# The order of SyncE's transfers in the first heads, and the tick tables of all background work, changed in an attention kernel with quantised feed-forward layers

## The chip, the core and the metric

The kernel runs on one core of a Trainium2 chip. Its time is the device time of one execution in microseconds, and the number given is the median of several runs. A core has five engines that run their own instruction streams and wait for one another by semaphores: TensorE (PE: matrix products and transposes, in the page also PEld, its weight loads), VectorE (DVE), ScalarE (ACT), GpSimd (POOL) and SyncE (SP), which here issues nearly all transfers between HBM and the on-chip memory.

## What is computed

Sixteen sequences of 512 rows by 128 columns go through three steps, each added to its input: half a feed-forward layer, attention with 16 heads of width 8, and half a feed-forward layer again. The feed-forward layer quantises its normed input and its weight in blocks of 32 to a grid of few values:

```
x = x + 0.5 * ffn(layernorm(x))
x = x + attn(layernorm(x))
x = x + 0.5 * ffn(layernorm(x))

# attn, for every head
scores = einsum('bhqd,bhkd->bhqk', Q, K) / sqrt(8)
mask   = sigmoid(tpms(position_q, position_k, phase[h]))
scores = scores + 0.3 * log(mask + 1e-06)
out    = einsum('bhqk,bhkd->bhqd', softmax(scores), V)

# ffn
scales = max(abs(block)) / 7.5
out    = (nearest_on_grid(block / scales) * scales) @ wd.T + bias
```

The mask depends on the head and the two positions alone, and so is the same for all sequences: 16 masks of 512 by 512, 1 MB each.

## The kernel before

**Batches, periods, heads, ticks.** The 16 sequences are four batches of four (NQ = QB = 4). A period is the attention of one batch: 16 heads, taken in the order of HEAD_ORDER (0, 8, 1, 2, 3, ...). Heads are counted through, m = 0 to 63, so head 16 opens period 1. A head has eight ticks, k = 0 to 7: for each of the four sequences j = k // 2 a half (pair = k % 2) of the keys. A period has 128 ticks, numbered through.

**A tick.** TensorE adds K times Q to the mask that already stands in a half of S_PS (`scores`, L1687), ScalarE takes the exponential of 1024 columns from it into E (`exp_step`, L803). In the odd ticks TensorE also multiplies a block of the head before with the values (`weighted`, L1705). In ticks 6 and 7 VectorE copies the next head's mask into the two halves of S_PS (`seed`, L1254), each after the exponential that frees the half. The passage from tick 7 to tick 0, with these copies, is called the seam here.

**Transfers of a head.** SyncE runs `head(m)` for each head: it loads the mask of head m + 1 (`load_mask`, L473, 1 MB, into one of two buffers LNM), its stack, six transfers of parts of K and Q (`load_stack`, L413 and L416, 672 KB together), and the two shift rows of the softmax (`load_shift`, L426). The stack of head m + 1 may be loaded when the scores of head m - 1 are done, its mask when head m is seeded. The last piece of a stack to be issued is the shift rows.

**The masks.** They are computed once, in the opening, in the order of MASK_ORDER, and are put where there is room: STAGE gives each a place in BIG, in memory that later belongs to something else. `store_mask(h)` (L458) brings mask h to HBM. What reuses the place waits for it: the exponentials of head 1 for masks 9 to 12, `load_mask(3)` for mask 8 (it stands in the buffer of the odd heads), the first `o_norm` for 13 and 14, the load of batch 2's rows for 15. Masks 0 and 8 are used in place by heads 0 and 1.

**Background work.** While a batch is in its period, the next two are prepared and the one before is finished, and each step of this is placed by a table: the step is issued in the tick that the table names, on its engine (the ending `_pe`, `_act`, `_ve`). FIRST prepares batch 1 in period 0, LATE the batches after it (in two halves), CHAINS gives the tick at which the chain of each sequence j starts and SECOND (CLOSE in period 0, APART in 1 and 2) the steps of a chain as distances from it, LAST the work after the attention. In a chain the normed rows are turned (`turn_pe`, TensorE), copied (`xnt_act`, ScalarE), multiplied to Q and K (`q_pe`, `k_pe`), copied again with their bias (`q_act`, `k_act`), split into three parts by VectorE and GpSimd (`hi_q_ve`, `mid_q_ve`, ...) and bounded (`norms_k_pe` to `bound_act`). LAST and LATE hold the layer norms and quantisation: statistics, `lnexp_act` and `rstd_ve` (three small instructions of VectorE, L1054 to L1056), `centre_ve` (subtract the mean, L1081), `reduce_ve`, `scales_ve`, `to_grid_ve`, `from_grid_ve`, then turn, copy, product and add. GpSimd has no table: it takes its steps in a fixed order, each as soon as what it waits for is there; its bias adds (L606) wait for the centring.

**What sets the order within a tick.** TensorE takes the background of ticks 0 and 1 ahead of the tick's scores, and that of ticks 2 to 7 behind the scores and values of the tick; so a step at tick 7 and one at tick 0 of the next head stand at the same place unless others are there. ScalarE takes it behind the exponential. VectorE has no tick of its own but the seeds: it works through what the tables name, in order, and only the seeds tie it to the other two.

## Time and profile before

| what | us |
|---|---|
| median of 3 runs | 866.96 |
| lowest and highest | 866.51, 867.02 |
| the profiled execution | 868.58 |
| its span | 866.7 |
| PE busy in the span | 730.6 (84%) |
| ACT busy | 645.3 (74%) |
| DVE busy | 560.7 (65%) |
| POOL busy | 190.4 (22%) |

The profiled execution has its own time, of which the span is the part between its first and last instruction. TensorE, busy for 84% of the span, reads as busy by modelled ends, so the share alone doesn't tell how near to its limit it is. The chain that ended last goes by PE for 48% of the span, by DVE for 23%, by ACT for 14%, by transfers for 2%.

### The profile page before, as it was taken

What the parts mean: (1) busy time and instruction counts of PE and PEld (TensorE: products, weight loads), DVE (VectorE), ACT (ScalarE), POOL (GpSimd) and SP (SyncE); (2) the same over time, 40 slices, a digit from 0 to 9 for tenths busy, and PEclk for the clock granted to TensorE, in tenths of its full rate; (3) what the DMA queues carried; (4) which work ended last, traced back from release to release, by engine and by line L of the source; (5) the groups of instructions that cost most, each with busy time, mean ns of one, the idle gap of its engine ahead of it and who ended that gap; (6) DMA issues with size and microseconds to landing.
All of it is one profiled execution on the core that took longest, in us unless ns stands there. A gap on an engine that the chain in (4) does not pass through costs nothing.

```text
span 866.7 us, 12515 instructions
## 1 busy us (share of the span) xinstructions
PE 730.6 (84%) x4195; PEld 247.8 (29%) x4195; DVE 560.7 (65%) x1385; ACT 645.3 (74%) x759; POOL 190.4 (22%) x163
## 2 busy tenths in 40 slices
PE   0575727899998999999999999999998998999935
PEld 0142311232232323332332233223311331331224
DVE  8968877466999646899774466886433457332274
ACT  1557596588887888878878888887888887888711
POOL 0405662003344203163140031441200002000011
PEclk9995956899999999999999999999999999999986
DMA  5527769874666674756867548668675556456101
GB/s 148 123 83 316 251 201 364 257 221 134 216 221 197 196 216 152 214 174 165 261 192 238 166 123 233 204 170 252 202 231 182 173 172 195 142 185 212 43 0 54
DMA packets 56075, 162.08 MB, mean 187 GB/s; under 512 B 14130, under 2 KB 24506, under 8 KB 45586
## 3 DMA queue, kind: packets, MB, share of 16 engines
q1 hardware_dynamic: 51780, 154.37, 58.0%
q0 software_dynamic: 1776, 5.93, 2.1%
q10 hardware_dynamic: 2446, 0.89, 0.5%
q8 instruction: 36, 0.59, 0.3%
q14 instruction: 37, 0.30, 0.1%
HBM read 117.86 MB, written 43.29 MB: 186 GB/s over the span
## 4 chain that ended last, share of the span: by engine, by line
PE 48%; DVE 23%; ACT 14%; issue 10%; DMA 2%; SPq 1%; POOL 1%; DVEq 0%; ACTq 0%; POOLq 0%
PE S_PS L1687 18%; PE O_PS L1705 17%; ACT BIG L803 10%; DVE S_PS L1254 7%; PE F_PS L1586 4%; PE F_PS L1581 2%; DMA BIG<-shift_rows 1%; ACT BIG L851 1%; PE R_PS L1715 1%; PE P_PS L1623 1%; DVE ST L981 1%; DVE SC L1091 1%; DVE BIG L1081 1%; PE P_PS L1581 1%; PE P_PS L1586 1%
## 5 line engine op out<-in xcount | busy, mean ns | idle before, releaser
L803 ACT ACTIVATE BIG<-S_PS 128x1024 f32<-128x1024 f32 x512 | 507.9, 1023 | 125.3 <-PE S_PS L1687 122.4
L1687 PE MATMUL S_PS<-BIG 98*128 98x512 bf16 x1024 | 313.0, 390 | 46.5 <-DVE S_PS L1254 19.7
L1254 DVE COPY S_PS<-BIG 128x512 f32<-128x512 f32 x256 | 159.6, 687 | 183.7 <-ACT BIG L803 181.5
L1705 PE MATMUL O_PS<-BIG,VXP 128*18 128x512 f32 (+2 forms) x2048 | 271.8, 604 | 0.0
L1687 PEld LDWEIGHTS S_PS<-BIG 98*128 98x128 bf16 x1024 | 79.2, 98 | 315.2 <-ACT BIG L803 138.6
L629 POOL TENSOR_TENSOR XDT<-PART 128x512 bf16<-128x512 f32 x24 | 28.8, 1200 | 296.2 <-ACT PART L766 296.2
L1705 PEld LDWEIGHTS O_PS<-BIG,VXP 128*18 128x18 f32 (+2 forms) x2048 | 34.3, 95 | 99.8 <-issue 96.0
L606 POOL TENSOR_TENSOR X<-X,BFH 128x512 f32<-128x512 f32 x16 | 24.0, 1527 | 146.6 <-DVE BIG L1081 117.2
L844 ACT ACTIVATE BIG<-S_PS,TEMP 128x1024 f32<-128x1024 f32 x32 | 34.2, 1111 | 20.2 <-PE S_PS L1880 19.6
L606 POOL TENSOR_TENSOR BIG<-BIG,BFH 128x512 f32<-128x512 f32 x16 | 19.9, 1274 | 122.9 <-DVE BIG L1081 110.9
L645 POOL TENSOR_TENSOR PART<-PART 128x512 bf16<-128x512 f32 x28 | 36.5, 1305 | 37.0 <-DVE PART L1162 37.0
L1880 PE MATMUL S_PS<-PART 36*128 36x512 bf16 (+1 forms) x32 | 14.7, 577 | 29.7 <-DMA PART<-trig_parts 27.6
L638 POOL TENSOR_TENSOR PART<-PART 128x512 f32<-128x512 f32 x28 | 35.1, 1252 | 13.2 <-DVE PART L1156 9.8
L735 ACT ACTIVATE XDT<-F_PS 128x512 f32<-128x512 f32 x38 | 22.5, 593 | 17.8 <-PE F_PS L1581 17.8
L1586 PE MATMUL F_PS<-WDT,XDT 128*128 128x128 f32 x208 | 32.2, 302 | 0.0
L1586 PEld LDWEIGHTS F_PS<-WDT,XDT 128*128 128x128 f32 x208 | 28.1, 207 | 12.6 <-ACT XDT L735 7.3
L851 ACT ACTIVATE BIG<-BIG,CON 128x2048 f32<-128x2048 f32 x16 | 30.7, 1988 | 0.0
L1581 PE MATMUL F_PS<-IDENT,BIG 128*128 128x128 f32 x112 | 17.9, 284 | 14.4 <-DVE BIG L1117 10.2
L1156 DVE CAST PART<-PART 128x512 bf16<-128x512 f32 x28 | 22.8, 813 | 5.1 <-ACT PART L766 4.4
L988 DVE TENSOR_SCALAR VE<-MV 128x4 f32<-128x4 f32 x48 | 22.7, 473 | 1.6
L729 ACT ACTIVATE RS<-VE 128x8 f32<-128x8 f32 (+1 forms) x19 | 4.0, 209 | 25.5 <-DVE VE L988 18.2
L981 DVE BATCH_NORM_STATS2 ST<-X 128x6 f32<-128x128 f32 x96 | 20.9, 280 | 0.6
(197 smaller groups left out, 745.2 us busy)
## 6 DMA issues: line engine op xcount, KB each, us to landing
BIG<-ln_masks SPq DMA_DIRECT2D x62, 1024.0 KB, 6.3
ln_masks<-BIG SPq DMA_DIRECT2D x16, 1024.0 KB, 6.2
BIG<-q_parts SPq DMA_DIRECT2D x63, 192.0 KB
BIG<-k_parts SPq DMA_DIRECT2D x63, 144.0 KB
BIG<-q_parts SPq DMA_DIRECT2D x63, 128.0 KB
q_parts<-PART SPq DMA_DIRECT2D x9, 768.0 KB, 3.8
k_parts<-PART SPq DMA_DIRECT2D x18, 384.0 KB, 4.4
BIG<-k_parts SPq DMA_DIRECT2D x63, 96.0 KB
```

The source lines that it names most:

```text
L606: pool.tensor_tensor(Y, Y, bias[:, None, :].to_broadcast((128, T, H)), ALU.add).then_inc(s[name], 1)
L638: pool.tensor_tensor(F_, F_, hi, ALU.subtract).then_inc(s[f"{q}_r1"], 1)
L645: pool.tensor_tensor(P_[2], F_, P_[1], ALU.subtract).then_inc(s[f"{q}_lo"], 1)
L803: act.activation(E[:, m % 2, j, 2 * pair:2 * pair + 2, :], S_PS[:, pair, :, :], ACT.Exp, scale=LOG_WEIGHT)\
L844: act.activation(stage(h)[:, 1024 * pair:1024 * pair + 1024].rearrange("p (k l) -> p k l", l=L), S_PS[:, t % 2, :, :], ACT.Sigmoid, scale= ...
L851: act.activation(a, a, ACT.Ln, bias=CON[:, 1:2]).then_inc(s["ln_mask"], 1)
L981: c(ve.bn_stats(ST[:, k, QB * j + t, :], xj[:, t, :]), wait=False)
L1254: ve.tensor_copy(S_PS[:, pair, i, :], LNM[:, slot, 2 * pair + i, :]).then_inc(s["seeded"], 1)
L1581: mm = pe.transpose(dst[:, 128 * t:128 * t + 128], src[:, t, :], IDENT[:, :])
L1586: mm = pe.matmul(dst[:, 128 * t:128 * t + 128], lhsT[:, 128 * t:128 * t + 128], rhs[:, :], start=True, stop=True)
L1687: mm = pe.matmul(S_PS[:, pair, i, :], KT[0:ALL_ROWS, slot, K_COL[j], 128 * kb:128 * kb + 128], QT[0:ALL_ROWS, slot, j, :], start=False, st ...
L1705: mm = pe.matmul(O_PS[32 * j:32 * j + ahead + HD + 1, :], VXP[:, slot_of(n), at - ahead:at + HD + 1], E[:, m % 2, j, kb, :], start=kb == 0 ...
```

## The change

It changes tables and the order of SyncE's calls; no instruction is added or removed, and what is computed is the same.

```diff
+AFTER = {1: (8,), 2: (13, 14), 3: (15,)}
...
-CHAINS = ((43, 59, 75, 91), (3, 27, 51, 75), (3, 27, 51, 75), ())
-APART = dict(norm_ve=-2, turn_pe=0, xnt_act=1, q_pe=5, q_act=5, ...
-CLOSE = APART | dict(k_pe=9, k_act=9, hi_k_ve=10, mid_k_ve=14, v_pe=13, v_ve=14)
+CHAINS = ((43, 59, 75, 91), (3, 27, 51, 83), (3, 27, 51, 91), ())
+CLOSE = dict(norm_ve=-2, turn_pe=3, xnt_act=3, q_pe=5, q_act=4, ...
+APART = dict(norm_ve=-2, turn_pe=0, xnt_act=0, q_pe=4, q_act=5, ...
...
                 if more and m >= 1:
                     load_mask(m + 1)
-                    if m == 1:
-                        for h in range(13, 15):
-                            store_mask(h)
                     load_stack(sp, m + 1)
                     if i < NH - 1:
                         load_shift(sp, m + 1)
-                if m == 2:
-                    store_mask(15)
-                    sp.wait_ge(s["val_ready"], 2 * HALF_TILES)
-                    load_x(3)
-                if m == 3:
+                for h in AFTER.get(m, ()):
+                    store_mask(h)
+                if m == 4:
                     lnm_stored(sp, 15)
                     load_x(2)
+                if m == 5:
+                    sp.wait_ge(s["val_ready"], 2 * HALF_TILES)
+                    load_x(3)
...
             store_mask(0)
 
-            store_mask(9)
-
             sp.wait_ge(s["bound_copied"], 1)
...
             load_stack(sp, 1)
-            store_mask(10)
+            store_mask(9)
             load_shift(sp, 1)
-            store_mask(11)
-            store_mask(12)
-            store_mask(8)
+            for h in range(10, 13):
+                store_mask(h)
```

On SyncE, from the store behind stack 1 to the load of mask 3 (`ln_masks<-BIG` is a store of a mask, `BIG<-ln_masks` a load, `k_parts`, `q_parts` and `shift_rows` are a stack). Before:

```order
L458 DMA ln_masks<-BIG 128x2048
L426 DMA BIG<-shift_rows 2x4x512
L458 DMA ln_masks<-BIG 128x2048 x3
L473 DMA BIG<-ln_masks 128x2048
L458 DMA ln_masks<-BIG 128x2048 x2
L413 DMA BIG<-k_parts 48x1536
L416 DMA BIG<-q_parts 48x2048
L413 DMA BIG<-k_parts 32x1x1536
L416 DMA BIG<-q_parts 32x1x2048
L413 DMA BIG<-k_parts 16x1x1536
L416 DMA BIG<-q_parts 16x1x2048
L426 DMA BIG<-shift_rows 2x4x512
```

After, with that file's line numbers (465 stores, 480 loads a mask, 420, 423 and 433 are the stack):

```order
L465 DMA ln_masks<-BIG 128x2048
L433 DMA BIG<-shift_rows 2x4x512
L465 DMA ln_masks<-BIG 128x2048 x3
L480 DMA BIG<-ln_masks 128x2048
L420 DMA BIG<-k_parts 48x1536
L423 DMA BIG<-q_parts 48x2048
L420 DMA BIG<-k_parts 32x1x1536
L423 DMA BIG<-q_parts 32x1x2048
L420 DMA BIG<-k_parts 16x1x1536
L423 DMA BIG<-q_parts 16x1x2048
L433 DMA BIG<-shift_rows 2x4x512
L465 DMA ln_masks<-BIG 128x2048
```

The two stores between the load of mask 2 and stack 2 (masks 13 and 14) are gone from there, and one store (mask 8) stands behind the stack. The first store is mask 10 before and 9 after, the three behind the shift rows are 11, 12 and 8 before and 10 to 12 after. The stores of 13 and 14 follow stack 3, that of 15 stack 4, the load of batch 2's rows stack 5 and of batch 3's rows stack 6; before, batch 3's followed stack 3 and batch 2's stack 4.

On ScalarE in head 16, the first of period 1, behind head 15: `PART<-P_PS` without BQK is the copy of the turned rows, `OTS<-O_PS` the copy of finished outputs that opens head 17. Before:

```order
L803 ACTIVATE BIG<-S_PS 128x1024 x8
L735 ACTIVATE PART<-P_PS 128x512
L803 ACTIVATE BIG<-S_PS 128x1024 x3
L812 ACTIVATE OTS<-O_PS,CON 128x512
L803 ACTIVATE BIG<-S_PS 128x1024
L766 ACTIVATE PART<-P_PS,BQK 128x512
```

After:

```order
L739 ACTIVATE PART<-P_PS 128x512
L807 ACTIVATE BIG<-S_PS 128x1024 x4
L816 ACTIVATE OTS<-O_PS,CON 128x512
L807 ACTIVATE BIG<-S_PS 128x1024
L770 ACTIVATE PART<-P_PS,BQK 128x512
```

The copy stands one exponential earlier, behind tick 3 and no more behind tick 4; TensorE's turn stays behind tick 3. Period 2 has the same at its opening.

On VectorE in period 3, from the statistics of head 53 to the seeds for head 55 (`COPY S_PS<-BIG`; L1081 is the centring, L1091 the reduction). Before:

```order
L988 TENSOR_SCALAR VE<-MV 128x4
L1254 COPY S_PS<-BIG 128x512 x4
L1081 TENSOR_TENSOR BIG<-BIG,MV 128x2048
L1054 TENSOR_TENSOR RS<-RS 128x16
L1055 SCALAR_TENSOR_TENSOR RS<-RS,VE 128x16
L1056 SCALAR_TENSOR_TENSOR RS<-RS 128x16
L1091 TENSOR_REDUCE SC<-BIG 128x64
```

After:

```order
L992 TENSOR_SCALAR VE<-MV 128x4
L1085 TENSOR_TENSOR BIG<-BIG,MV 128x2048
L1258 COPY S_PS<-BIG 128x512 x4
L1095 TENSOR_REDUCE SC<-BIG 128x64
L1058 TENSOR_TENSOR RS<-RS 128x16
L1059 SCALAR_TENSOR_TENSOR RS<-RS,VE 128x16
L1060 SCALAR_TENSOR_TENSOR RS<-RS 128x16
```

The centring stands ahead of the seeds for head 54, and the reduction ahead of the three rstd instructions.

Of the other moves, those of which more is said below, by period and tick (k is the tick in the head):

| step | engine | before | after |
|---|---|---|---|
| period 0, four chains: turn, copy | PE, ACT | k = 3, 4 | k = 6, 6 |
| period 0: copy of Q | ACT | k = 0 of the next head | k = 7 |
| period 1: turns of `turn_pe` 18 and `turn_xd_pe` 82, 98 | PE | k = 2 | 17, 81, 97, k = 1 |
| period 2: turns of 18, 82, 90 | PE | k = 2 | 15, 80, 87, k = 7, 0, 7 |
| periods 1, 2: last chain starts | all | 75 | 83, 91 |
| periods 1, 2: `norms_q_pe` | PE | k = 6 | k = 5 |
| period 2, head 38: centring, rstd | DVE | 49, 50 | 50, 49 |
| period 3: `add_ve` of the third sequence | DVE | 33, head 52 | 31, head 51 |

## Rows read from the trace of the kernel before

**Rows 1.** The page's part 5, the costliest group.
```profile
L803 ACT ACTIVATE BIG<-S_PS 128x1024 f32<-128x1024 f32 x512 | 507.9, 1023 | 125.3 <-PE S_PS L1687 122.4
```
**Rows 2.** Windows: length; busy us (instructions) of PE, PEld, DVE, ACT, POOL; clock, DMA, GB/s.
```profile
240.00:260.00 20.00, 19.29 (x115) 7.34 (x113) 18.05 (x56) 16.47 (x24) 8.48 (x8) 1.00 0.68 212
...
720.00:740.00 20.00, 16.97 (x96) 3.52 (x88) 18.39 (x24) 14.35 (x16) 4.98 (x4) 0.91 0.56 175
```
**Rows 3.** Timeline of SyncE's queue, 127 to 143: start, us, instruction, tiles, count.
```profile
127.23 0.44 SPq L458 DMA_DIRECT2D ln_masks<-BIG  x1
...
128.40 3.81 SPq L458 DMA_DIRECT2D ln_masks<-BIG  x3
132.74 0.75 SPq L473 DMA_DIRECT2D BIG<-ln_masks  x1
133.55 2.69 SPq L458 DMA_DIRECT2D ln_masks<-BIG  x2
136.29 1.41 SPq L413 DMA_DIRECT2D BIG<-k_parts  x1
...
142.37 0.64 SPq L426 DMA_DIRECT2D BIG<-shift_rows  x1
```
**Rows 4.** The chain of waits in order of time: start, us, what.
```profile
142.37 12.48 DMA BIG<-shift_rows
```
**Rows 5.** Transfers by line in 127:136, 132:152, 169:192.5; issue to landing.
```profile
L458 SPq DMA_DIRECT2D ln_masks<-BIG x6: 440/1250/1403, 127.2 to 134.8; - x6
DMA to landing us min/median/max: 5.9/9.0/15.0
...
L473 SPq DMA_DIRECT2D BIG<-ln_masks x3: 468/752/2656, 132.7 to 151.7; - x3
DMA to landing us min/median/max: 12.1/15.0/20.4
...
L473 SPq DMA_DIRECT2D BIG<-ln_masks x3: 338/338/877, 169.5 to 191.9; - x3
DMA to landing us min/median/max: 5.0/9.6/13.8
```
**Rows 6.** Timeline of TensorE where heads 2, 4 and 7 start; last: idle before, releaser.
```profile
154.90 1.89 PE L1687 MATMUL S_PS<-BIG 98*128 98x512 bf16 x4 [7.55 <-DMA BIG<-shift_rows]
...
178.61 0.60 PE L1687 MATMUL S_PS<-BIG 98*128 98x512 bf16 x2
...
210.30 0.60 PE L1687 MATMUL S_PS<-BIG 98*128 98x512 bf16 x2
```
**Rows 7.** Timelines of TensorE and ScalarE in head 16.
```profile
316.82 0.66 PE L1581 MATMUL P_PS<-IDENT,XC 128*128 128x128 f32 x4
...
320.43 0.60 PE L1687 MATMUL S_PS<-BIG 98*128 98x512 bf16 x2 [0.58 <-ACT BIG L803]
...
318.86 0.59 ACT L735 ACTIVATE PART<-P_PS 128x512 f32<-128x512 f32 x1
```
**Rows 8.** Timeline of TensorE, first score products of heads 46 and 47.
```profile
642.11 0.89 PE L1687 MATMUL S_PS<-BIG 98*128 98x512 bf16 x2 [0.52 <-DVE S_PS L1254]
...
651.79 0.89 PE L1687 MATMUL S_PS<-BIG 98*128 98x512 bf16 x2 [0.53 <-DVE S_PS L1254]
```
**Rows 9.** Timeline of VectorE in head 38.
```profile
557.77 2.29 DVE L1081 TENSOR_TENSOR BIG<-BIG,MV 128x2048 f32<-128x2048 f32 x1
...
561.46 1.21 DVE L1054 TENSOR_TENSOR RS<-RS 128x16 f32<-128x16 f32 x1
```
**Rows 10.** Timeline in period 3: product of head 51, rstd of 54, seam and values of 55.
```profile
700.53 1.16 PE L1586 MATMUL F_PS<-WO,XDT 128*128 128x128 f32 x8
...
724.56 0.17 DVE L1054 TENSOR_TENSOR RS<-RS 128x16 f32<-128x16 f32 x1
...
731.73 0.89 PE L1687 MATMUL S_PS<-BIG 98*128 98x512 bf16 x2 [1.87 <-DVE S_PS L1254]
...
733.96 1.93 PE L1705 MATMUL O_PS<-BIG,VXP 128*27 128x512 f32 x8
```

More of the change, by code:

```diff
@@ new lines @@
+LATE = ((dict(stats_ve=(49, 52), lnexp_act=59, rstd_ve=60, centre_ve=64, reduce_ve=67, scales_ve=68, to_grid_ve=73,
+              from_grid_ve=77, turn_pe=(81, 87), xd_copy_act=(83, 89), ffn_pe=(84, 93), add_ve=(85, 93), stats1_ve=(90, 96),
+              lnexp1_act=98, rstd1_ve=98),
+         dict(stats_ve=(82, 83), lnexp_act=87, rstd_ve=91, centre_ve=97, reduce_ve=99, scales_ve=100, to_grid_ve=106,
+              from_grid_ve=106, turn_pe=(109, 118), xd_copy_act=(109, 118), ffn_pe=(112, 120), add_ve=(113, 122),
+              stats1_ve=(113, 122), lnexp1_act=123, rstd1_ve=125)),
+        (dict(stats_ve=(26, 27), lnexp_act=31, rstd_ve=32, centre_ve=33, reduce_ve=35, scales_ve=36, to_grid_ve=42,
+              from_grid_ve=42, turn_pe=(47, 58), xd_copy_act=(47, 58), ffn_pe=(54, 60), add_ve=(53, 61), stats1_ve=(57, 66),
+              lnexp1_act=68, rstd1_ve=75),
+         dict(stats_ve=(76, 81), lnexp_act=83, rstd_ve=86, centre_ve=89, reduce_ve=91, scales_ve=91, to_grid_ve=96,
+              from_grid_ve=99, turn_pe=(110, 118), xd_copy_act=(110, 118), ffn_pe=(113, 120), add_ve=(113, 121),
+              stats1_ve=(114, 122), lnexp1_act=125, rstd1_ve=123)))
@@ L125 @@
-LAST = ({}, AMID, AMID, ALONE)
+LAST = ({},
+        dict(turn_pe=(10, 17, 25, 31), at_act=(10, 18, 26, 34), out_pe=(12, 20, 28, 36), add_ve=(13, 21, 29, 37),
+             stats_ve=(16, 24, 29, 43), lnexp_act=45, centre_ve=51, rstd_ve=51, reduce_ve=56, scales_ve=60, to_grid_ve=64,
+             from_grid_ve=72, turn_xd_pe=(75, 81, 86, 97), xd_copy_act=(75, 81, 87, 97), ffn_pe=(77, 83, 92, 100),
+             add_ffn_ve=(77, 85, 91, 101)),
+        dict(turn_pe=(10, 15, 26, 34), at_act=(10, 18, 26, 34), out_pe=(12, 20, 30, 36), add_ve=(13, 21, 27, 37),
+             stats_ve=(18, 24, 32, 40), lnexp_act=49, centre_ve=50, rstd_ve=49, reduce_ve=56, scales_ve=57, to_grid_ve=65,
+             from_grid_ve=72, turn_xd_pe=(75, 80, 87, 98), xd_copy_act=(75, 80, 87, 98), ffn_pe=(77, 84, 94, 100),
+             add_ffn_ve=(75, 85, 96, 97)),
+        dict(turn_pe=(14, 22, 30, 38), at_act=(14, 22, 30, 38), out_pe=(15, 24, 32, 39), add_ve=(18, 25, 31, 40),
+             stats_ve=(18, 26, 36, 42), lnexp_act=51, centre_ve=43, rstd_ve=51, reduce_ve=48, scales_ve=54, to_grid_ve=58,
+             from_grid_ve=62, turn_xd_pe=(62, 70, 78, 86), xd_copy_act=(62, 70, 78, 86), ffn_pe=(64, 72, 80, 88),
+             add_ffn_ve=(67, 75, 85, 92)))
```

39 lines of the change are left out of this document (11 added, 28 removed).

## Prediction

> **What bounds the kernel now.** I read the page's busiest groups first, then the windows, then the chain of waits, then the timelines of the places where the change moves something. The costliest group is the exponentials, 512 of 1.02 us, eight to a head (L803), whose idle time ends with TensorE's scores (L1687) [rows 1]. A head on which nothing else lies takes 9.68 us, from its first score product at 642.11 to the next one at 651.79 [rows 8]. 64 such heads are 620 us of the span of 866.7 us. The rest is the opening, the ending, the background work of the other batches, and one hole: at 154.90 TensorE takes up head 2 after 7.55 us without work [rows 6], and the chain of waits puts the 12.48 us before it on the load of the shift rows, which is the last piece of that head's stack [rows 4].
>
> Why was that load late? SyncE issued it at 142.37 [rows 3], behind a queue: stores of masks 10 (127.23), 11, 12 and 8 (three from 128.40), the load of mask 2 (132.74), stores of 13 and 14 (133.55), then the stack (136.29). The landings come in that order. The last of the six stores was issued at 134.8 and landed 15.0 us later, at 149.8; mask 2's load landed at 132.7 + 12.1 = 144.8 [rows 5]. So two stores took 5.0 us of queue, 2.5 each, and the stack another 5.1 (149.8 to 154.9).
>
> **The stall (term A).** The new order has no store of 13 and 14 ahead of stack 2, and mask 8's store goes behind it; mask 9's store comes in after stack 1 instead, so mask 2's load has the same number of stores ahead since 127 and should land at 144.8 as now. Stack 2 can be issued when head 0's scores are done, about 134.8, and lands at 144.8 + 5.1 = 149.9: 5.0 us earlier. But the stores are only moved, and the queue has to carry them later. From the mask loads: mask 3 landed at 143.1 + 15.0 = 158.1 and mask 4 at 151.7 + 20.4 = 172.1; mask 5 at 169.5 + 13.8 = 183.3 and mask 6 at 180.7 + 9.6 = 190.3 [rows 5]. Between the last two lie one stack and one load, 7.0 us. Between the first two lie a stack, a store and two loads, 14.0 us, which leaves about 8 for a stack and a load. I take 7.5 for a head (3.5 the load, 4.0 the stack) and 3.5 for a batch of x, which has a mask's size. The new queue after stack 2 at 149.9 is then: mask 8 stored, 152.4. SyncE stands in mask 3's load until that has landed, and behind it stand stack 3, the stores of 13 and 14, and all later loads. The fastest load of the rows takes 5.0 us, so mask 3 lands at 157.4 and stack 3 at 161.4. Masks 13 and 14 to 166.4, head 4's pair to 173.9; mask 15 and head 5's pair to 183.9; batch 2 of x and head 6's pair to 194.9; batch 3 of x and head 7's pair to 205.9. Heads 4 and 7 now start at 178.61 and 210.30 [rows 6]. So of the 5.0 us, 4.7 are left at head 4 and 4.4 at head 7. From head 8 on the queue has no extra transfers, and with heads of 10.6 us (178.61 to 210.30 is three) it regains 3 us in each. **A = 4.4 us**; from 2.8 (below) to 5.5, if the stack takes 4.6.
>
> The other waits on the moved transfers are covered: head 1's exponentials need stores 9 to 12, which land at the places where 10, 11, 12 and 8 land now (133.1 for the first, 127.2 + 5.9 [rows 5]), and one tick's pair of score products and exponentials later each; the first o_norm needs 13 and 14 in head 4, 10 us after they land.
>
> **The tick tables.** In a period TensorE and ScalarE alternate. A background step costs what it adds to the engine that is late. Three kinds of moves count.
>
> *Copy right behind its turn.* In head 16, TensorE turns the normed rows at 316.82 (0.49 us to the next start), but ScalarE copies them only after one more exponential, at 318.86, and TensorE then stands 0.58 us before the score product at 320.43 [rows 7]. With the copy one tick earlier it lies in the time in which ScalarE waits for the turn anyway. That gives 0.5 us for the first chain of batches 2 and 3 each; the other chains stand beside a product of 1 us that covers the copy, and I take nothing for them. In batch 1's four chains the turn goes to tick k = 6, the copy beside it, and the Q copy into the gap at the head's end.
>
> *Turns into the head's seam.* At the seam TensorE waits for VectorE's mask copies: 0.52 us before the first score product of head 46, and again between its products [rows 8]. A turn (about 0.45 us) set at k = 7, 0 or 1 fills that; at k = 2 it is paid. With the last chain moved away (75 to 83 and 91), period 1 has three such turns (of 17, 81, 97) and period 2 three (15, 80, 87): 1.3 us each.
>
> *VectorE's order.* Centring 2048 columns takes 2.29 us, and it sets off GpSimd's bias adds; the small rstd step behind it then takes 1.21 us [rows 9], where the same instruction takes 0.17 us alone [rows 10]. In head 38 the new order puts the three rstd steps ahead of the centring. In head 54, centring, rstd, reduction and scales all stand between two seeds, and the seeds for head 55 are late: TensorE waits 1.87 us instead of 0.53, and then a group of value products takes 1.93 us, the granted clock of the slice being 0.91 [rows 2, 10]. The new order centres in head 53, where VectorE has room.
>
> Sums. **B**, period 0 behind head 7: four chains at 0.6 us at most, 2.4. But the first is under the queue's limit above, and the others lie where VectorE is busy 18.05 of 20 us [rows 2] with the same work as now, so 1.0 (0 to 2.4). **C**, period 1: 0.5 + 1.3 + 0.6 for head 28's late seed, whose chain steps go to head 28 and 29: 2.4 (0 to 4). **D**, period 2: 0.5 + 1.3 + 0.9 (head 38's 3 us of VectorE bring about 0.4 at the seam, and norms_q one tick earlier 0.5): 2.7 (0 to 3.5). **E**, period 3: 1.3 + 0.9 for the slow clock, less 0.8 for a new wait: an add now stands between the two pairs of seeds for head 52 and waits for a product that TensorE runs after head 51's last scores and values. That product took 1.16 us at 700.53 [rows 10]; with the add behind it the second pair comes some 1.3 us later than now, and the seam's own wait of 0.5 covers a part. 1.4 (-0.8 to 2.2).
>
> 4.4 + 1.0 + 2.4 + 2.7 + 1.4 = 11.9 us. The profiled execution took 868.58 us, 1.9 more than its span, and the median of the runs is 866.96, 1.6 below it. 868.6 - 11.9 = 856.7 for a profiled run, so **855.1 us** in the median.
>
> **A rule on GpSimd.** The seeds and casts that the tables move meet GpSimd's work at other moments. The rstd instruction at 1.21 and 0.17 us [rows 9, 10] shows what one such meeting costs: 1 us. The Trainium skill (GPSIMD Engine Reference, section Specifications) says that GpSimd's interfaces to SBUF are shared with VectorE and contend with its instructions that have two SBUF inputs; by that rule, which these rows bear out, every reordering may lose as well as win. Ten more such meetings before seeds that are already late would cost 10 us and undo B to E; that is why their lower ends are at 0.
>
> **Rivals.** *Only the stall pays* (0.16): VectorE is the bound of periods 0 to 2 and what TensorE saves returns as waiting for seeds. For it: seeds that follow VectorE's work without a gap before heads 10, 12, 13, 22, 23. Against it: heads 16, 32 and 54, where VectorE or ScalarE is free. 866.96 - 4.4 = 862.6.
>
> *The stack passes the stores anyway* (0.12): if the stack's late landing is its own and not the queue's, only SyncE's earlier issue counts: the shift rows go out some 2.8 us before 142.37 (two stores of 1.3 us each, and less waiting). A = 2.8 or less, with B to E cut by a third: 859. The Trainium skill (DMA: Bandwidth & Descriptors, Queues, rings and completion order) says that completion is not first-in first-out for an issuing engine, since a transfer may use fewer rings than another. The nine landings above are all in the order of issue, which speaks against it here.
>
> *All of it pays* (0.17): the upper ends, and the clock does not fall at head 2: 5.5 + 2.0 + 3.5 + 3.3 + 2.2 = 16.5, 850.5.
>
> *The queue falls behind* (0.05, slower). Place: SyncE waiting in mask 3's load for mask 8's store, with everything for heads 3 to 7 behind it. Price: six stacks at 5.1 instead of 4.0 and seven loads at 4.3 instead of 3.5 add 12 us, and head 7 starts 7.6 us later than now; with B to E at nothing the time is 874. It decides from head 7's stack landing after 210.3 plus what B to E bring; at 7.5 of those it would only be 867.
>
> *Nothing measurable* (0.03): half of that, or A undone by B to E.
>
> **How the numbers follow.** The forecast has 0.47. A measurement of this kernel can tell about 0.2% (1.7 us) from no change. Faster: 0.47 + 0.16 + 0.12 + 0.17 = 0.92; same 0.03; slower 0.05. The range reaches from the full case to the one where only the stall pays: 849.5 to 863.5.
>
> **What would show it.** After: head 2's first score product near 149.9 with under 3 us of idle before it; mask 3's load issued near 152 and not at 143; heads 4 and 7 at 173.9 and 205.9. In head 16 no wait of 0.58 us at its end. Head 54 to 55 with 0.5 us of wait and full clock; a wait of VectorE between the seeds of head 52. I am wrong if head 2 still waits over 4 us, if heads 3 to 7 wait for shift rows beyond these times, or if the seeds of periods 1 and 2 come later than now.

## Result and the profile after

| | median, us | lowest and highest | profiled execution | its span |
|---|---|---|---|---|
| before, 5 runs | 867.02 | 866.51, 872.70 | 868.58 | 866.7 |
| after, 5 runs | 855.03 | 849.15, 856.45 | 849.15 | 846.9 |

The ratio is 0.9846, with a 95% interval of 0.9814 to 0.9879: faster by 1.5%. The changed kernel was measured twice more among the experiments, with ratios of 0.983 (0.9803 to 0.9858) and 0.9831 (0.9804 to 0.9858), so some 12 to 15 us. Its profiled execution is the shortest of its five, 5.9 us under their median, and is no measure of the whole; its parts are compared below with two further profiles.

From the page of the changed kernel: the busy times, the chain that ended last, and the costliest group (line 807 is line 803 of before, 1691 is 1687):

```profile
PE 721.2 (85%) x4195; PEld 246.6 (29%) x4195; DVE 544.2 (64%) x1385; ACT 644.1 (76%) x759; POOL 193.1 (23%) x163
...
PE 46%; DVE 18%; ACT 17%; issue 9%; DMA 5%; SPq 3%; POOL 1%; DVEq 0%; ACTq 0%; POOLq 0%
...
L807 ACT ACTIVATE BIG<-S_PS 128x1024 f32<-128x1024 f32 x512 | 505.0, 1023 | 108.1 <-PE S_PS L1691 105.2
```

The first of these lines in the kernel before:

```profile
PE 730.6 (84%) x4195; PEld 247.8 (29%) x4195; DVE 560.7 (65%) x1385; ACT 645.3 (74%) x759; POOL 190.4 (22%) x163
```

The exponentials take the same 1.02 us each, and ScalarE waits 108.1 us for scores where it waited 125.3 [rows 1]. The surprise is in the busy times: VectorE executes the same 1385 instructions in both kernels, and was busy for 560.7 us before and 544.2 after. Its share of the chain fell from 23% to 18%, that of transfers rose from 2% to 5%.

The start of a head is the start of its first score product on TensorE. This table gives the time between such starts, in us, for the profiles that are compared whole; e1 to e12 are the experiments below. Because heads repeat to within some 0.01 us from one execution to another except at a few places, a difference of 0.1 us in a period can be read.

| profile | start of head 0 | 0 to 8 | 8 to 16 | 16 to 32 | 32 to 48 | 48 to 63 | from 63 to the end |
|---|---|---|---|---|---|---|---|
| before | 126.3 | 95.0 | 90.5 | 176.7 | 172.9 | 150.2 | 55.0 |
| after | 121.8 | 89.8 | 87.8 | 173.2 | 169.2 | 148.4 | 56.7 |
| after, second profile (e1) | 125.4 | 88.8 | 87.9 | 173.5 | 169.2 | 148.4 | 54.3 |
| after, third profile (e12) | 124.5 | 90.1 | 87.1 | 177.0 | 169.4 | 148.5 | 54.6 |
| order alone (e2) | 124.1 | 90.2 | 90.5 | 176.7 | 172.9 | 150.0 | 55.0 |
| tables alone (e3) | 126.6 | 94.6 | 87.1 | 175.5 | 169.2 | 148.5 | 54.0 |
| before, small bias adds (e9) | 125.8 | 95.3 | 90.0 | 174.4 | 170.8 | 147.5 | 53.6 |
| after, small bias adds (e10) | 123.5 | 89.7 | 86.3 | 173.5 | 169.7 | 148.5 | 53.4 |

**The stall.** SyncE's queue in the changed kernel, from the three stores behind shift rows 1 to shift rows 3 (start, us, instruction):

```profile
126.10 3.18 SPq L465 DMA_DIRECT2D ln_masks<-BIG  x3
129.40 1.16 SPq L480 DMA_DIRECT2D BIG<-ln_masks  x1
131.02 0.83 SPq L420 DMA_DIRECT2D BIG<-k_parts  x1
...
137.01 0.64 SPq L433 DMA_DIRECT2D BIG<-shift_rows  x1
137.70 0.39 SPq L465 DMA_DIRECT2D ln_masks<-BIG  x1
146.65 0.34 SPq L480 DMA_DIRECT2D BIG<-ln_masks  x1
...
150.76 0.64 SPq L433 DMA_DIRECT2D BIG<-shift_rows  x1
```

and TensorE where heads 2, 3 and 4 start (in brackets idle before, and what ended it):

```profile
144.36 1.04 PE L1691 MATMUL S_PS<-BIG 98*128 98x512 bf16 x4 [2.00 <-DMA BIG<-shift_rows]
...
155.61 0.60 PE L1691 MATMUL S_PS<-BIG 98*128 98x512 bf16 x2 [2.09 <-DMA BIG<-shift_rows]
...
169.05 0.60 PE L1691 MATMUL S_PS<-BIG 98*128 98x512 bf16 x2 [0.27 <-DMA BIG<-shift_rows]
```

Head 2 waits 2.00 us instead of 7.55 [rows 6]. Its shift rows take 7.35 us from issue to use, where it was 12.48 [rows 4]. As forecast, SyncE then stands in the load of mask 3 for mask 8's store, from 137.7 to 146.65, with stack 3 behind it, and head 3 waits 2.09 us for its shift rows. (That the one causes the other is tested in e5.)

**The opening.** Head 0 started 4.5 us earlier, which the prediction did not have at all. 1.7 us of it are the change. In the opening GpSimd stores the last K parts and may load head 0's stack only when they have landed. The transfer view of before in 112 to 120 us, and of after in 109 to 117 (queue, count, KB, us from issue to landing):

```profile
ln_masks<-BIG SPq DMA_DIRECT2D x1, 1024.0 KB, 4.0
...
k_parts<-BIG POOLq DMA_DIRECT2D x1, 384.0 KB, 4.5
```

```profile
k_parts<-BIG POOLq DMA_DIRECT2D x1, 384.0 KB, 2.9
```

Before, SyncE issued a store of a mask at 114.10 and GpSimd its K parts at 114.63; both ran together and the K parts took 4.5 us. The new order has put that store behind stack 1, and they take 2.9. From the last product of the opening to head 0's first scores it takes 8.2 us in before, 6.5 in after, 6.4 in e1 and 6.6 in e2. (That the moved store does this is shown by e4. The way from the K parts to the scores is read from the trace only: there the wait that ends last is for shift rows that SyncE loads beside GpSimd's loads of the stack.) The other 2.85 us are no effect of the change. The same instructions ran slow for longer in before; its TensorE, and then that of after:

```profile
52.07 1.91 PE L1586 MATMUL P_PS<-WDT,XDT 128*128 128x128 f32 x8
```

```profile
46.68 1.45 PE L1590 MATMUL F_PS<-WDT,XDT 128*128 128x128 f32 x8
...
50.03 1.16 PE L1590 MATMUL P_PS<-WDT,XDT 128*128 128x128 f32 x8
```

By their durations, eight such products take 1.91 us at the lower of TensorE's two levels (1.2 GHz) and 1.16 at the upper (2.4 GHz); the durations alone tell this, for the granted clock is given as 1.00 in both traces here. In after the rise came in the middle of the group at 46.68, in before behind the one at 52.07. In the later profiles of the changed kernel head 0 started at 125.4 and 124.5, so this was chance.

**Head 16** (ScalarE and TensorE of after, to be read against [rows 7]):

```profile
303.61 0.65 PE L1585 MATMUL P_PS<-IDENT,XC 128*128 128x128 f32 x4
304.10 1.03 PE L1691 MATMUL S_PS<-BIG 98*128 98x512 bf16 x4
```

```profile
304.30 0.60 ACT L739 ACTIVATE PART<-P_PS 128x512 f32<-128x512 f32 x1
304.80 3.82 ACT L807 ACTIVATE BIG<-S_PS 128x1024 f32<-128x1024 f32 x4
```

The copy starts 0.7 us behind its turn (303.61 to 304.30), four exponentials follow it without a gap, and the wait of 0.58 us is gone.

**Heads 52 to 55.** Head 52 takes 11.02 us instead of 10.07, head 54 9.74 instead of 11.02 and head 55 10.56 instead of 12.00. The forecast wait between the pairs of seeds is there (VectorE of after; L1284 is the add):

```profile
680.17 1.29 DVE L1258 COPY S_PS<-BIG 128x512 f32<-128x512 f32 x2 [5.13 <-ACT BIG L807]
682.00 0.69 DVE L1284 TENSOR_TENSOR BIG<-F_PS,BIG 128x512 f32<-128x512 f32 x1 [0.54 <-PE F_PS L1590]
682.61 1.28 DVE L1258 COPY S_PS<-BIG 128x512 f32<-128x512 f32 x2
```

and at head 55 the stall and the slow value products of [rows 10] are gone (TensorE of after):

```profile
711.66 0.89 PE L1691 MATMUL S_PS<-BIG 98*128 98x512 bf16 x2 [0.35 <-DVE S_PS L1258]
...
713.67 1.06 PE L1709 MATMUL O_PS<-BIG,VXP 128*27 128x512 f32 x8
```

### The profile page after: what moved, and what is told of

Its sections match the earlier page's. It is cut to its first block, busy times and chain, and to the rows that moved or that the text cites. A ratio compares the mean times of both kernels' runs of the same rounds, so it can differ in the third digit from the quotient of the medians.

```text
span 846.9 us, 12510 instructions
## 1 busy us (share of the span) xinstructions
PE 721.2 (85%) x4195; PEld 246.6 (29%) x4195; DVE 544.2 (64%) x1385; ACT 644.1 (76%) x759; POOL 193.1 (23%) x163
## 4 chain that ended last, share of the span: by engine, by line
PE 46%; DVE 18%; ACT 17%; issue 9%; DMA 5%; SPq 3%; POOL 1%; DVEq 0%; ACTq 0%; POOLq 0%
PE S_PS L1691 18%; PE O_PS L1709 17%; ACT BIG L807 12%; DVE S_PS L1258 6%; DMA BIG<-shift_rows 5%; PE F_PS L1590 3%; ACT BIG L855 2%; DVE ST L985 2%; SPq L420 2%; SPq L423 1%; PE R_PS L1719 1%; PE F_PS L1585 1%; PE P_PS L1631 1%; PE P_PS L1627 1%; PE P_PS L1590 1%
## 5 line engine op out<-in xcount | busy, mean ns | idle before, releaser
L807 ACT ACTIVATE BIG<-S_PS 128x1024 f32<-128x1024 f32 x512 | 505.0, 1023 | 108.1 <-PE S_PS L1691 105.2
L1691 PE MATMUL S_PS<-BIG 98*128 98x512 bf16 x1024 | 304.9, 388 | 39.2 <-DVE S_PS L1258 13.1
L848 ACT ACTIVATE BIG<-S_PS,TEMP 128x1024 f32<-128x1024 f32 x32 | 34.3, 1112 | 16.5 <-PE S_PS L1884 16.0
L642 POOL TENSOR_TENSOR PART<-PART 128x512 f32<-128x512 f32 x28 | 35.0, 1251 | 11.8 <-DVE PART L1160 8.6
L739 ACT ACTIVATE XDT<-F_PS 128x512 f32<-128x512 f32 x38 | 22.7, 596 | 16.8 <-PE F_PS L1585 16.5
L1129 DVE TENSOR_TENSOR BIG<-F_PS,BIG 128x512 f32<-128x512 f32 x14 | 9.6, 685 | 18.3 <-PE F_PS L1590 18.3
```

Of the source, the lines that this page charges most:

```text
L642: pool.tensor_tensor(F_, F_, hi, ALU.subtract).then_inc(s[f"{q}_r1"], 1)
L807: act.activation(E[:, m % 2, j, 2 * pair:2 * pair + 2, :], S_PS[:, pair, :, :], ACT.Exp, scale=LOG_WEIGHT)\
L848: act.activation(stage(h)[:, 1024 * pair:1024 * pair + 1024].rearrange("p (k l) -> p k l", l=L), S_PS[:, t % 2, :, :], ACT.Sigmoid, scale= ...
L1691: mm = pe.matmul(S_PS[:, pair, i, :], KT[0:ALL_ROWS, slot, K_COL[j], 128 * kb:128 * kb + 128], QT[0:ALL_ROWS, slot, j, :], start=False, st ...
```

## Experiments

### The changed kernel again (e1, e12)

No edit.

> The changed kernel once more, unedited. Its profiled execution took 849.15 us while the median of its runs was 855.03. Theory 1 (the opening's clock is chance): in the first profile TensorE's clock rose at about 48 us against 54 in the kernel before, which brought 2.85 us, with the same instructions in both; another profile will show a rise near 54 in about half of the cases, head 0 starting at about 124.6 instead of 121.8, and the median stays at 854 to 856. Theory 2 (the new order brings the early rise): every profile of this kernel starts head 0 at 121.8 and the profiled time is 849 to 850 again. In both, heads 8 to 63 take the same time as in the first profile, 590.2 us from the start of head 8 back to front: head 8 to head 63 in 578.6 us (211.58 to 790.18), within 0.5.

853.43 us in the median of 6 (849.85 to 856.15), just under the 854 to 856 expected. Head 0 started at 125.4, so an early opening is not the new order's. Where TensorE's rise lies was guessed wrongly: by the durations it came early here too, at about 49 us, and the gain was lost again behind it: from 94 to 104 us the granted clock was 0.50 in e1 and 1.00 in after. Head 8 to head 63 took 579.1 us, as expected.

> The changed kernel a third time, unedited, as the measure beside the kernel with both mends. The median of its two measurements was 855.03 and 853.43, the profiled executions 849.15 and 849.85. Theory: median 853 to 856; from head 8 to head 63 578.5 to 579.5 us in the profile, the spread of the runs lying in the opening and in the ending, where TensorE's clock rises and falls at other moments. Rival: the spread lies in the periods, where VectorE and GpSimd meet at other moments, and head 8 to 63 comes out at 580 or more.

853.14 us (851.41 to 856.62), profiled 853.79. Here the rival is right in its number and not in its cause: head 8 to 63 took 582.0 us, 3.4 more than in the first profile, but VectorE met GpSimd as often as there (18 long small instructions, counted below). The excess lies in head 22 (12.21 instead of 11.48 us), head 25 (12.40 instead of 11.43) and head 26 (13.09 instead of 11.50). TensorE at the start of head 26, in e12 and then in after:

```profile
413.95 0.60 PE L1691 MATMUL S_PS<-BIG 98*128 98x512 bf16 x2 [2.22 <-DMA BIG<-shift_rows]
...
416.19 1.93 PE L1709 MATMUL O_PS<-BIG,VXP 128*27 128x512 f32 x8
```

```profile
409.12 0.60 PE L1691 MATMUL S_PS<-BIG 98*128 98x512 bf16 x2 [1.25 <-DMA BIG<-shift_rows]
...
410.96 1.06 PE L1709 MATMUL O_PS<-BIG,VXP 128*27 128x512 f32 x8
```

A new wait stands there that the kernel before does not have: head 26 waits for its stack. Head 23 has another such wait, 0.71 us in after and 1.45 in e12, which is the excess of head 22. With 2.22 us of it the value products behind take 1.93 us instead of 1.06, and the granted clock of 412 to 420 us is 0.79 against 1.00 around the same place in after:

```profile
412.00:420.00 8.00, 6.05 (x32) 1.93 (x32) 5.25 (x20) 4.40 (x7) 0.00 (x0) 0.79 0.99 260
```

```profile
408.00:416.00 8.00, 6.88 (x48) 3.49 (x48) 5.83 (x21) 6.46 (x11) 0.00 (x0) 1.00 0.98 253
```

The wait is in all nine profiles of kernels with the new tables and full bias adds, 1.2 to 2.7 us; in the three where it was longest (1.98 in e3, 2.22 in e12, 2.69 in e11) head 26 took 13.1 us, in the six others 11.5 to 11.8. Heads 25 and 26 make 1.9 of the 3.9 us by which e12's profiled execution is longer than e1's (853.79 and 849.85). How often the long wait comes in executions that were not profiled is not known.

### SyncE's order alone (e2), the tables alone (e3)

e2 is the changed kernel with the tables of before, e3 the kernel before with the new tables.

> SyncE's new order with all tick tables of the kernel before. My theory: the order brings the stall at head 2 (4.4 us in the prediction, about 5 by the trace of the changed kernel) and about 1.7 us in the opening that the prediction did not have, since the last K parts of the opening are stored in 2.9 us instead of 4.5 us once mask 9's store no longer runs beside them; median 860.5 to 862.5. From head 8 on, head for head, the times of the kernel before within 0.3 us in total. Rival (the queue takes it back): the transfers moved behind stacks 3 to 6 make heads 3 to 7 later, so that at head 8 less than 3 us is left and the median is at 864 to 866. Second rival (order and tables need each other): at head 16 the advance is gone because VectorE bounds period 0, median 865 to 867.

861.54 us (858.06 to 864.93), ratio 0.9925 (0.9897 to 0.9952). From the start of head 0 to that of head 8 4.9 us less than before, in the opening 1.6 less, and behind head 8 nothing: 90.5, 176.7 and 172.9 us to the tenth. The gain of the queue is neither given back nor added to behind head 8, so both rivals are out.

> All new tick tables with SyncE's order of the kernel before. My theory: the tables bring 1.0 + 2.4 + 2.7 + 1.4 = 7.5 us by the prediction, 2.7 + 3.6 + 3.7 + 1.8 = 11.8 us by the trace of the changed kernel (read at heads 8, 16, 32, 48 and 63); median 855.5 to 859.5, and the stall at head 2 as in the kernel before, 7 to 8 us before the first score product of head 2, which starts near 155. Rival (the two interact: the later start of head 2 leaves VectorE more time, so that period 0 gains nothing behind head 8): median 859 to 862.

857.71 us (851.03 to 858.89), ratio 0.9855 (0.9819 to 0.9891). Head 2 started at 155.45 behind the old stall. From 8 to 16 3.5 us less than before, 1.2 from 16 to 32 (here head 26's wait took its share), 3.7 from 32 to 48, 1.7 from 48 to 63, 10.1 in all. Between the starts of heads 0 and 63 the order alone brings 5.1 us and the tables alone 10.6, in all 15.7, and the whole change brings 13.3 to 17.5 in its three profiles. As far as this spread tells, the two halves are independent.

### One store moved alone (e4)

```diff
             store_mask(0)
-            store_mask(9)
...
             load_stack(sp, 1)
-            store_mask(10)
+            store_mask(9)
             load_shift(sp, 1)
+            store_mask(10)
             store_mask(11)
```

> The kernel before with one edit: the store of mask 9 is taken from ahead of the opening's last steps and put behind stack 1, the stores of 10, 11, 12 and 8 in their order behind it; 13 and 14 stay ahead of stack 2. My theory: the K parts stored last in the opening (issued at 114.6 us) land in 2.9 us instead of 4.5 us, head 0 starts 1.7 us earlier, but the queue ahead of stack 2 is as long as before (five stores, the load, two stores: one more than now behind 127 us), so that head 2 starts no earlier than 154.9 and 0 to 2.5 us later; median 867 to 869.5. Rival (the opening's gain is passed on): the queue runs from an earlier point and all is earlier by 1.7, median 865.3.

870.85 us in the median of 12, ratio 1.0032 (1.0014 to 1.005): slower, by a little more than expected. The K parts landed in 2.9 us and it took 6.4 us from the opening's last product to head 0, so this store alone makes the opening's 1.7 us. (Head 0 started only 0.75 us earlier than in before, at 125.57, as TensorE was slower further ahead.) But head 2 started 31.8 us behind head 0 instead of 28.6: one more store stands ahead of stack 2. The opening's gain is worth something only because the same change shortens the queue elsewhere.

### Stack 3 ahead of mask 3 (e5)

```diff
-                    load_mask(m + 1)
+                    if m != 2:
+                        load_mask(m + 1)
                     load_stack(sp, m + 1)
                     if i < NH - 1:
                         load_shift(sp, m + 1)
+                    if m == 2:
+                        load_mask(m + 1)
```

> The changed kernel with stack 3 ahead of the load of mask 3. In its trace SyncE stands in that load from 137.7 to 146.6, until mask 8's store has landed, with stack 3 behind it, and head 3 then waits 2.09 us for its shift rows. My theory (the queue stands idle behind the waiting load): stack 3 is issued as soon as head 1's scores are done, near 22 us after the start of head 0, mask 3 lands when it did, and head 3's wait of 2 us goes; from the start of head 0 to that of head 4 it takes 45.0 to 45.7 us instead of 47.2, of which at least 1 us is left at head 8 (88.8 to 89.8 us now). Median 852 to 854. Rival (the mask takes the stack's place as the late one): mask 3 lands 3.5 us later behind the stack, the seeds of head 3 wait for it, and head 4 starts no earlier; median as that of the changed kernel.

850.44 us (844.77 to 856.18), ratio 0.9802 (0.976 to 0.9844). Stack 3 was issued from 143.7 and its shift rows at 147.31, mask 3's load at 149.27. Head 0 to head 4 took 44.5 us instead of 47.1 to 47.6, head 0 to head 8 86.1 instead of 88.8 to 90.1: more than expected. So the waiting load did hold up stack 3. What is late at head 3 now is what the rival named, the seeds, for which VectorE waited 3.27 us for mask 3; but they cost less (TensorE of e5):

```profile
156.91 0.89 PE L1694 MATMUL S_PS<-BIG 98*128 98x512 bf16 x2 [0.97 <-DVE S_PS L1261]
```

### The add at tick 33 again (e6)

```diff
-        dict(turn_pe=(14, 22, 30, 38), ..., add_ve=(18, 25, 31, 40),
+        dict(turn_pe=(14, 22, 30, 38), ..., add_ve=(18, 25, 33, 40),
```

> The changed kernel with the add of the third sequence in period 3 put back from tick 31 to tick 33. By the prediction's term E the add at tick 31 stands between the two pairs of seeds for head 52 and costs up to 0.8 us. Head 52 took 10.07 us before and 11.02 after the change. My theory: head 52 takes 10.0 to 10.1 again, no other head changes by over 0.1, head 48 to head 63 in 147.4 to 147.6 us instead of 148.41. Rival: the 0.95 us comes from other steps of head 51 and 52 that moved (the product one tick earlier, its copy), and head 52 stays at 11.0.

851.16 us (849.41 to 853.42), ratio 0.9804 (0.9776 to 0.9832). Head 52 took 10.06 us, head 48 to 63 147.50, and no other head of period 3 changed by over 0.04. The 0.95 us of head 52 are this one add.

### The copy one tick later, the turns at k = 2 (e7, e8)

```diff
-APART = dict(norm_ve=-2, turn_pe=0, xnt_act=0, q_pe=4, ...
+APART = dict(norm_ve=-2, turn_pe=0, xnt_act=1, q_pe=4, ...
```

> The changed kernel with the copy of the turned rows (xnt_act) in periods 1 and 2 one tick later again, as before the change. By the prediction it costs 0.5 us in head 16 and 0.5 in head 32 and nothing for the other chains: head 16 10.3 to 10.4 us instead of 9.8 to 9.9, head 32 10.9 to 11.1 instead of 10.4 to 10.6, in all 1.0 us. Rival 1: the copy costs nothing there, since the products behind it were moved too, 0 to 0.2 us in all. Rival 2: each of the eight chains pays, 2 to 4 us in all.

One execution, 855.5 us. The border between heads 15 and 16 itself moves by 0.7 us from profile to profile, so the two are taken together: 20.28 us, against 19.84, 19.89 and 19.84 in the three profiles of after. Heads 31 and 32 together 20.27, against 19.82 to 19.83. So the copy is worth 0.45 us in each of the two, and nothing in most others, as forecast. Head 38 took 12.16 us instead of 10.6 to 10.8, which none of the theories had; VectorE's seeds for head 39 waited there for their mask:

```profile
553.56 2.47 DVE L1258 COPY S_PS<-BIG 128x512 f32<-128x512 f32 x4 [2.87 <-DMA BIG<-ln_masks]
```

Whether the copy made that load late or chance did, one profile does not tell.

e8 sets the first turns at 18 in both periods, the others at 82, 98 and 82, 90, 98, and the product at 84.

> The changed kernel with the six turns that it set at k = 7, 0 or 1 in periods 1 and 2 (at 17, 81, 97 and 15, 80, 87) back at k = 2 as before (18, 82, 98 and 18, 82, 90), and the product at 83 back at 84. By the prediction each costs 0.44 us there: 1.3 us in period 1 (heads 18, 26, 28) and 1.3 in period 2 (heads 34, 42, 43). Rival 1: at k = 2 TensorE is not the late one either, since VectorE's seeds set the pace of these heads: under 0.5 us in all. Rival 2: the copies that now stand a tick behind their turns matter more, over 4 us in all.

One execution, 853.1 us. Period 1: head 18 11.83 us instead of 11.55, head 26 11.51 instead of 11.50, head 28 11.80 instead of 11.52, in all 0.6 us. Period 2: heads 34, 42 and 43 longer by 0.28, 0.44 and 0.45, head 33 shorter by 0.44, in all 0.7. That is half of the 1.3 forecast for each, and neither rival. One profile stands behind it, and head 22 was 0.3 us longer too, by its wait for a stack.

### VectorE and GpSimd (e9, e10)

Behind 126 us, VectorE has 163 small instructions of the groups statistics (L988), rstd (L1054 to L1056), scales (L1097 to L1101 without the reciprocal, L1099) and bounds (L1200, L1208, L1210). In before they take 0.1 to 0.4 us, or 0.86 to 1.24, and nothing between. Sorted by whether a tensor instruction of GpSimd ran at the same time:

| profile | none beside it, all short | one beside it, short | one beside it, over 0.5 us |
|---|---|---|---|
| before | 113 | 14 | 36 |
| order alone (e2) | 112 | 14 | 37 |
| tables alone (e3) | 132 | 14 | 17 |
| after | 132 | 13 | 18 |
| before, small bias adds (e9) | 128 | 16 | 18 |
| after, small bias adds (e10) | 138 | 15 | 9 |

Not one was long without GpSimd. (The last two profiles have records of 162.) The 36 long ones of before took 38.8 us, the 18 of after 16.9. The experiment makes the bias adds small:

```diff
-                pool.tensor_tensor(Y, Y, bias[:, None, :].to_broadcast((128, T, H)), ALU.add)...
+                pool.tensor_tensor(Y[:, :, 0:1], Y[:, :, 0:1], bias[:, None, 0:1].to_broadcast((128, T, 1)), ALU.add)...
```

> The kernel before, with GpSimd's bias adds (L606) made on 1 of 128 columns: so most of the two biases b_ffn and bo is left out of the result. What is tested is the meeting of VectorE with GpSimd: in the trace of before, 36 of 163 small instructions of VectorE (statistics, rstd, bounds, scales) behind 126 us took over 0.5 us, each of them while an instruction of GpSimd ran, and in half of these it was a bias add; none of the 113 that ran beside no instruction of GpSimd did. My theory (the tables gain by fewer meetings): heads 22 and 38, where four small instructions in a row took 1.0 to 1.2 us beside bias adds, fall from 12.83 to 10.9 to 11.6 us and from 11.47 to 10.3 to 10.8; heads 54 and 55, with two such in front of the seeds, from 23.0 to 20.5 to 21.5; head 41 stays at 12.55 and head 12 at 13.3, since what they wait for isn't a bias add. From head 8 to head 63 584 to 587 us instead of 590.3. Rival (the meetings are beside the path, the turns and the moved chain are the gain): heads 22 and 38 change by under 0.5 us, head 8 to 63 over 588.5.

One execution, 859.16 us, beside 868.42 for the kernel before on that chip. VectorE in head 22, in before (GpSimd's four bias adds ran from 384.20 to 389.16) and then in e9:

```profile
384.52 0.98 DVE L1210 TENSOR_TENSOR BMAX<-BMAX 128x1 f32<-128x1 f32 x1
385.53 1.21 DVE L1054 TENSOR_TENSOR RS<-RS 128x16 f32<-128x16 f32 x1
386.77 1.20 DVE L1055 SCALAR_TENSOR_TENSOR RS<-RS,VE 128x16 f32<-128x16 f32 x1
388.00 1.19 DVE L1056 SCALAR_TENSOR_TENSOR RS<-RS 128x16 f32<-128x16 f32 x1
```

```profile
382.88 0.21 DVE L1210 TENSOR_TENSOR BMAX<-BMAX 128x1 f32<-128x1 f32 x1
383.12 0.17 DVE L1054 TENSOR_TENSOR RS<-RS 128x16 f32<-128x16 f32 x1
383.33 0.17 DVE L1055 SCALAR_TENSOR_TENSOR RS<-RS,VE 128x16 f32<-128x16 f32 x1
383.54 0.18 DVE L1056 SCALAR_TENSOR_TENSOR RS<-RS 128x16 f32<-128x16 f32 x1
```

4.58 us become 0.73. With full adds each of the four small steps ends as one of the bias adds does. Head 8 to head 63 took 582.7 us instead of 590.3, more than expected. Head 38 fell to 10.66 and heads 54 and 55 from 23.0 to 20.3 us, which is what the change itself made of them; head 22 only to 11.98. Head 12 stayed at 13.35 as expected. Head 41 did not stay, it fell to 11.73: ahead of its seeds a bound step (L1200) had met a bias add, 1.20 us and now 0.20.

The edit does one thing more than end the meetings: GpSimd's four adds take 0.66 us instead of 4.96, so that its other work and what waits for it may come earlier. Where the small steps themselves are shown to shrink, as in heads 22, 38 and 54, the meetings are the cause; for the sum over all heads the two are not separated.

> The changed kernel with the same edit, bias adds on 1 of 128 columns, most of both biases left out. My theory: the new tables had already taken most meetings away (18 of 163 small instructions over 0.5 us, ten of them beside a bias add), so the edit brings less than in the kernel before: from head 8 to head 63 577.5 to 578.8 us instead of 579.1 (578.6 in the other profile), and the difference between the two kernels there falls from about 11.5 to 6 to 8.5 us. Rival (what the tables gain has nothing to do with GpSimd): both kernels gain the same and the difference stays at 11 to 12 us.

One execution, 847.18 us; head 8 to 63 577.9, against 578.6, 579.1 and 582.0 in the three profiles of the changed kernel. The two kernels lie 4.8 us apart there with small bias adds, and 8.4 to 11.7 with full ones. So 43 to 59% of what the tables gain goes with the bias adds, more than I had expected.

### Both mends (e11)

> Both mends of the changed kernel together: stack 3 ahead of the load of mask 3 (alone it brought 2.6 us between the starts of heads 0 and 4) and the add of the third sequence in period 3 back at tick 33 (alone it brought 0.95 us in head 52). Theory: they lie in different places and add up, 3 to 4 us under the changed kernel measured beside it, head 0 to head 8 in 86.0 to 87 us, head 52 in 10.06; median 848.5 to 851. Rival: the early gain is given back behind head 8, as the other meetings of VectorE fall differently there, and the median is within 1.5 us of the changed kernel's.

852.54 us (846.55 to 852.91), ratio 0.9797 (0.9769 to 0.9826), 0.6 us under the changed kernel measured beside it (0.9831). Head 52 took 10.07 us, but the rest of the expectation fell: head 0 to head 8 took 89.7 us and not 86 to 87. The rival's median came true, though not its place: the gain was given back ahead of head 8. Up to head 4 all was as in e5 (44.2 us). Then heads 5 and 6 waited for their stacks, which in e5 they did not:

```profile
180.74 1.04 PE L1694 MATMUL S_PS<-BIG 98*128 98x512 bf16 x4 [1.81 <-DMA BIG<-shift_rows]
...
193.27 1.89 PE L1694 MATMUL S_PS<-BIG 98*128 98x512 bf16 x4 [2.56 <-DMA BIG<-shift_rows]
```

The batches of x are transferred just there; the transfers of the core were at 100% in 170 to 193 us and moved 250 GB/s, against 98% and 258 in the same stretch of e5 (169 to 192). So the gain was lost to a queue that is nearly full in every profile of the new order (93% or more in 170 to 193 us); why it fell behind here and not in e5, these profiles don't show. No version here beats the changed kernel by more than the spread of its runs: e5, e6 and e11 have the lower medians, but their intervals overlap with those of e1 and e12.

## Why the prediction was right, and where not

The time came out at 855.03 us where 855.1 was forecast, and 853.1 to 853.4 in two more measurements. The stall was right in its mechanism; of what the tables gained, about half came by a mechanism that the sum hardly had. The agreement to the tenth is luck, since terms that were too small and effects that were left out cancelled.

**A, the stall: right.** 4.4 us forecast, 4.9 measured at head 8 where it stands alone (e2), 4.6 at head 7. The chain of its steps can be read off, counted from head 0: head 2 was to start after 23.6 us (149.9 less 126.3) and did after 22.6; mask 3's load was to be issued after 25.7 and was after 24.9 (146.65 less 121.80); heads 4 and 7 were to start after 47.6 and 79.6 and did after 47.3 and 79.0. One piece was wrong: mask 2's load landed 19.6 us after head 0's start and not 18.5 as before, and the stack behind it needed 3.0 us (141.4 to 144.36) and not 5.1, so head 2 gained more than the 5.0 forecast, 5.8 in e2. Masks 13, 14 and 15 and both batches of x then cost the later heads 1.2 us of that by head 7, where the sum had 0.6. The rival that the stack passes the stores is out, and so is the one that the queue falls behind.

**The opening: left out.** The prediction counted the stores behind 127 us and took mask 9's store out from ahead of the opening's last steps without asking who shares the transfers there: 1.7 us. The row was in the same view, the store's issue at 114.10 beside GpSimd's at 114.63.

**B, period 0: the term was too small, and its reason wrong.** 1.0 forecast, 2.6 to 3.5 measured. The step that failed is "the others lie where VectorE is busy 18.05 of 20 us [rows 2] with the same work as now". The work was the same and its time was not. Heads 8 to 15 in both kernels (first before, then after; the third figure with a count is VectorE):

```profile
221.40:311.90 90.50, 85.32 (x513) 27.80 (x511) 75.28 (x185) 74.37 (x99) 31.89 (x25) 1.00 0.68 206
```

```profile
211.60:299.40 87.80, 84.69 (x513) 27.80 (x511) 72.10 (x185) 74.22 (x101) 34.02 (x25) 1.00 0.71 212
```

The largest part is head 12, 13.35 to 10.67 us. Between its two groups of seeds VectorE does the same instructions in both kernels, in 11.8 us before and 9.0 after. Two casts and two steps of the scales, which GpSimd's instructions had overlapped, make the difference (before, then after, one cast and the two steps):

```profile
276.66 1.26 DVE L1156 CAST PART<-PART 128x512 bf16<-128x512 f32 x1
277.85 1.15 DVE L1097 TENSOR_TENSOR SC<-SC,RS 128x32 f32<-128x32 f32 x1
279.03 1.07 DVE L1098 TENSOR_SCALAR SC<-SC 128x32 f32<-128x32 f32 x1
```

```profile
264.24 0.19 DVE L1101 TENSOR_TENSOR SC<-SC,RS 128x32 f32<-128x32 f32 x1
264.47 0.18 DVE L1102 TENSOR_SCALAR SC<-SC 128x32 f32<-128x32 f32 x1
265.84 0.43 DVE L1160 CAST PART<-PART 128x512 bf16<-128x512 f32 x1
```

These meetings are with GpSimd's steps on Q and K and not with its bias adds, so that e9 leaves them as they are; no run takes them away alone.

**C and D, periods 1 and 2.** C: 2.4 forecast, 3.6, 3.2 and -0.3 in the three profiles. D: 2.7 forecast, 3.7, 3.6 and 3.5. Of their parts, the copy was 0.5 and is 0.45 twice (e7), the turns 1.3 each and are 0.6 and 0.7 (e8). What makes up for it was hardly in the sum. Head 38 fell from 11.47 to 10.6 to 10.75: none of its four small steps meets a bias add any more, and e9 gives the same (10.66); I had 0.4 for it. Head 22 fell from 12.83 to 11.5: there two of the four small steps still meet a bias add (1.15 and 1.20 us in after), and e9, which ends all four meetings, brings 0.85 us, so the rest has another cause. Head 41 fell from 12.55 to 10.71, of which e9 shows 0.8 as a meeting; the other 1.0 us is only argued to be the chain that now starts later and is no more in this head. The largest gain of period 1, head 27 (11.99 to 10.49), no run takes apart. Against these stands head 26's wait for its stack; the prediction had named such waits as a sign of being wrong, but for heads 3 to 7 alone.

**E, period 3: right by its parts.** 1.4 forecast, 1.8 measured: heads 54 and 55 give 2.7 us (1.3 + 0.9 forecast). With small adds (e9) they give 2.7 in the old order too: there the rstd steps need 2.0 us less, and VectorE then stands idle for 0.7 us before the seeds. In the changed kernel both these meetings and the centring, 2.29 us, are gone from between the seeds; either would do, and no run separates them. The add costs 0.95 (0.8 forecast; e6).

**The rule on GpSimd: about half of the tables' gain, and I had used it only for the lower ends.** The 1.21 us that I cited was one of 36, and their sum was to be had from the trace of before. The 0.17 us that I called the step's time alone [rows 10] was the first of three, begun 0.05 us before a bias add; the two behind it took 1.15 and 1.20. By them a table that keeps VectorE's small steps out of GpSimd's instructions could gain up to 36 times 0.9, 32 us of VectorE's time; with the new tables its busy time fell by 16.5, from 560.7 to 544.2 us (559.4 in e2, 544.1 in e3). The Trainium skill (SBUF — State Buffer, SBUF: two separate sides) calls the pair of ports that the two share an exclusive lock, held for a whole instruction, by which the other "fully blocks". The rows agree: in head 22 each of four small steps takes 1.0 to 1.2 us, which is up to the end of a bias add (1.24 us each, a quarter of 4.96).

**The sum.** 1.7 (opening) + 4.9 + 3 + 3 + 3.6 + 1.8 are 18 us in a good execution, where 11.9 were forecast; that is nearer to the rival *All of it pays* (16.5, though its 2.0, 3.5 and 3.3 for B, C and D are not the upper ends that the sums give, 2.4, 4 and 3.5). The medians show 12 to 15. In an execution such as e12's the waits at heads 23 and 26 and the clock behind the second take 3.3 of this; the rest was not taken apart: the unprofiled executions have no traces, and the opening and the ending differ by up to 3.6 and 2.4 us between the three profiles of the changed kernel.

## What to carry to other kernels

Where two engines share something, a step's price depends on what the other does at that moment: sort the durations of one small instruction, and if they have two levels, count the long ones and look at what they run beside before any table is set anew. When transfers are moved out of one queue's way, look at every stretch that they leave and enter, also before the place that the change is about; here, where the transfers took 90% or more of the time, the shorter heads waited for their stacks at new places. And compare part by part: parts that repeat to 0.01 us, as most heads do here, show in one profile what a median of runs can't.
